# Flags by a line in DRAM, and an earlier third mask, in an adaLN block on one core

## What is computed

```python
mod = (silu(c) @ wmod).reshape(2, 6, 1, -1)          # c is [2, 512]
sa, ca, ga, sb, cb, gb = (mod[:, i] for i in range(6))
ga, gb = guarded(ga), guarded(gb)                     # sign(g) * max(|g|, 0.25)
h = layernorm(x) * (1 + ca) + sa
keep = mask.reshape(16, 32, 16, 32).sum((1, 3)) > 0   # one answer per 32x32 block
x = x + ga * (h @ (weight * expand(keep)).T)
h = layernorm(x) * (1 + cb) + sb
g = silu(h @ Wg.T * ag); u = h @ Wu.T * au            # 1376 inner features
x = x + gb * ((g * u) @ Wd.T * ad)
```

## Time and profile before

| | us |
|---|---|
| median of 3 runs (lowest, highest) | 177.42 (176.82, 177.63) |
| the profiled execution, its own time | 176.95 |
| its span (first to last instruction) | 175.2 |
| PE busy in the span | 168.9 (96%) |
| DVE, ACT, POOL busy | 100.1, 81.7, 29.8 |
| DMA traffic | 23.73 MB |

### The profile page before, as it was taken

One profiled execution on the slowest core, in us unless ns is written; L12 is line 12 of the kernel. 1 busy time (PEld: TensorE's weight loads), 2 busy tenths in 40 slices (PEclk: granted clock), 3 DMA queues, 4 the chain that ended last, 5 costly groups with the idle time before them and its releaser, 6 DMA issues.

```text
span 175.2 us, 2553 instructions
## 1 busy us (share of the span) xinstructions
PE 168.9 (96%) x899; PEld 128.8 (74%) x899; DVE 100.1 (57%) x204; ACT 81.7 (47%) x115; POOL 29.8 (17%) x40
## 2 busy tenths in 40 slices
PE   6889999999999999999999999999999999999992
PEld 6855555375568887887788888888888888888881
DVE  6776862894594998324755564427644213442574
ACT  3034002578996957756466443553435524352200
POOL 1333620591049320000000000006500000000000
PEclk9999999999999999999999999999999999999999
DMA  5999997999959402331300000001500000000014
GB/s 175 358 404 402 409 292 241 412 409 404 400 174 314 134 0 50 88 78 31 123 0 6 0 4 0 4 0 60 185 4 0 4 0 4 0 6 0 4 60 180
DMA packets 12389, 23.73 MB, mean 135 GB/s; under 512 B 2920, under 2 KB 5232, under 8 KB 11856
## 3 DMA queue, kind: packets, MB, share of 16 engines
q1 hardware_dynamic: 10864, 22.03, 34.7%
q10 hardware_dynamic: 1504, 1.39, 2.6%
HBM read 19.48 MB, written 2.10 MB: 123 GB/s over the span
## 4 chain that ended last, share of the span: by engine, by line
PE 79%; DMA 7%; SPq 6%; DVE 4%; POOL 1%; issue 1%; ACT 0%; DVEq 0%; POOLq 0%
PE bank L915 46%; PE bank L985 20%; PE bank L883 8%; DMA maskt<-in_att_mask 5%; DMA wffn<-wffn 2%; SPq L241 2%; PE bank L971 2%; PE bank L790 2%; PE bank L862 1%; SPq L263 1%; SPq L256 1%; SPq L250 1%; SPq L253 1%; POOL awork L343 1%; DVE wffn L562 1%
## 5 line engine op out<-in xcount | busy, mean ns | idle before, releaser
L915 PE MATMUL bank<-ht,whi_gu 128*128 128x512 f32 x352 | 83.6, 391 | 0.0
L915 PEld LDWEIGHTS bank<-ht,whi_gu 128*128 128x128 f32 x352 | 65.6, 188 | 13.9 <-issue 0.5
L678 DVE SCALAR_TENSOR_TENSOR awork<-bank,scal,awork 128x512 f32<-128x512 f32 x22 | 16.5, 751 | 50.6 <-PE bank L915 48.2
L985 PE MATMUL bank<-whi_dn,in_split 128*128 128x512 f32 x148 | 37.3, 391 | 0.0
L492 ACT ACTIVATE awork<-bank,scal 128x512 f32<-128x512 f32 x22 | 15.2, 690 | 46.0 <-PE bank L915 46.0
L985 PEld LDWEIGHTS bank<-whi_dn,in_split 128*128 128x128 f32 x148 | 27.6, 188 | 5.9
L883 PE MATMUL bank<-awork,wffn 128*128 128x512 f32 x64 | 31.1, 606 | 0.4 <-ACT wffn L421 0.2
L440 ACT ACTIVATE whi_gu<-wffn 128x1024 fp32r<-128x1024 f32 x22 | 23.3, 1058 | 6.9 <-PE bank L915 6.9
L883 PEld LDWEIGHTS bank<-awork,wffn 128*128 128x128 f32 x64 | 10.7, 190 | 9.9 <-issue 7.4
L687 DVE TENSOR_TENSOR in_split<-awork,in_split 128x512 fp32r<-128x512 f32 x21 | 16.5, 786 | 0.7
L433 ACT ACTIVATE junk<-wffn 128x1536 uint8<-128x1536 uint16 x11 | 16.2, 1477 | 0.9 <-DMA wffn<-in_w_down 0.9
(11 more groups left out here) (72 smaller groups left out, 113.6 us busy)
## 6 DMA issues: line engine op xcount, KB each, us to landing
wffn<-in_w_gu SPq DMA_DIRECT2D x10, 512.0 KB, 8.6
wffn<-in_w_down SPq DMA_DIRECT2D x10, 256.0 KB, 9.4
xt<-in_x SPq DMA_DIRECT2D x8, 256.0 KB, 6.4
modw<-in_mod_ln SPq DMA_DIRECT2D x4, 512.0 KB, 7.3
modw<-in_mod_gate SPq DMA_DIRECT2D x2, 1024.0 KB, 9.6
modw<-in_mod_ln SPq DMA_DIRECT2D x2, 1024.0 KB, 9.2
maskt<-in_att_mask SPq DMA_DIRECT2D x4, 256.0 KB, 8.1
awork<-in_att_w SPq DMA_DIRECT2D x4, 256.0 KB, 8.1
```

The costliest lines, as they stand in the source:

```text
L678: dve.scalar_tensor_tensor(inner[:, s % 2, :], bank[gu_bank(s, 1)][:, :], scal[:, c, 1:2], silu_g[:, s % 2, :], ALU.mult, ALU.mult).then_i ...
L915: return pe.matmul(bank[gu_bank(s, u)][:, :], w, h, start=(k == 0 and part == 0), stop=(k == KT - 1 and part == 1))
L985: last = pe.matmul(bank[4 + t][:, :], h, w, start=(c == 0 and part == 0), stop=(c == C - 1 and part == 1))
```

## The change

It has four parts.

1. SP loads mask 2 ahead of the last two x tiles. DVE sums it behind the first statistics of batch 1 and makes keep behind the second. PE's `mask_blocks(2)` stands behind the fourth product of k = 0 instead of the first of k = 1. POOL multiplies the weights of slice 2 ahead of batch 1's first deviation. Epsilon is added by DVE, inside `stats`, behind every second tile, for all norms.
2. ACT copies gate 0 ahead of modulation 4, and the first of the checks moves from behind modulation 7 to behind modulation 5. DVE makes the first layer's four gate products of batch 0 ahead of the second turned block.
3. The flags of groups 1 and 2 no longer go through PE. `flag_vector` runs in steps 2 and 5; SP writes the column to a line in DRAM (128 rows of 4 bytes), waits until it has landed, and reads the line back into one partition (512 bytes); DVE reduces that line to its maximum and compares it, in steps 3 and 6. PE's two flag sums go; its flag loads stay where they were. On SP the first of these pairs stands behind the weight chunks' loads and ahead of the 16 block moves, the second behind these moves and ahead of the gate line.
4. Step 1 has two checks instead of one, and step 5 none instead of one.

```diff
--- before.py
+++ after.py
@@ -61,7 +61,9 @@
 HALF = D // 2
 SHIFT = BLK + NB
 
-CHECKS_AT = {0: 1, 1: 1, 2: 1, 3: 1, 4: 1, 5: 1}
+CHECKS_AT = {0: 1, 1: 2, 2: 1, 3: 1, 4: 1}
+FLAG_VECTOR_AT = {2: 1, 5: 2}
+FLAG_READ_AT = {3: 1, 6: 2}
 
 GROUPS = [(0, 4), (4, C - HELD), (C - HELD, C)]
 GROUP_OF = [g for g, (a, b) in enumerate(GROUPS) for _ in range(a, b)]
@@ -119,7 +121,10 @@
         mhalf = sb("mhalf", [P, TT])
         chk = sb("chk", [P, C])
         flagv = sb("flagv", [P, len(GROUPS)])
+        flagrow = sb("flagrow", [1, len(GROUPS), P])
+        flagmax = sb("flagmax", [1, len(GROUPS)])
         flags = sb("flags", [1, len(GROUPS)], I32)
+        flag_line = nc.dram_tensor("flag_line", (len(GROUPS), P), F32, kind="Internal").ap()
 
         gates = maskt[:, :, :].bitcast(F32)
 
@@ -212,6 +217,9 @@
         flagv_ok = sem("flagv_ok")
         flag_done = sem("flag_done")
         flag_ok = sem("flag_ok")
+        d_flag_out = sem("d_flag_out")
+        d_flag_in = sem("d_flag_in")
+        flagmax_ok = sem("flagmax_ok")
         wgu_hi = sem("wgu_hi")
         wd_hi = sem("wd_hi")
         gate_mm = sem("gate_mm")
@@ -269,9 +277,11 @@
             load_ln1(2)
             load_mask(1)
             load_att(1)
-            for t in range(TT, NB * TT):
-                load_x(t)
+            load_x(TT)
+            load_x(TT + 1)
             load_mask(2)
+            load_x(TT + 2)
+            load_x(TT + 3)
             load_att(2)
             load_ln1(3)
             sp.dma_start(modw[:, 2, :, :], mod_gate[0]).then_inc(d_gate[0], 16)
@@ -299,11 +309,19 @@
                                  w_gu_tail).then_inc(d_ffn[c], 16)
                     sp.dma_start(wffn[0:FT, c, 2 * D:3 * D], w_down[c * P:F, :])\
                       .then_inc(d_ffn[c], 16)
+            def turn_flag(g):
+                sp.wait_ge(flagv_ok, g + 1)
+                sp.dma_start(flag_line[g], flagv[:, g:g + 1]).then_inc(d_flag_out, 16)
+                sp.wait_ge(d_flag_out, 16 * g)
+                sp.dma_start(flagrow[0:1, g, :], flag_line[g:g + 1, :]).then_inc(d_flag_in, 16)
+
+            turn_flag(1)
             sp.wait_ge(xn_ok, XN_FIRST + 3 * TT)
             for j in range(P // BLK):
                 for i in range(P // BLK):
                     sp.dma_start(modw[BLK * j:BLK * (j + 1), 1, :, i * P:(i + 1) * P],
                                  modw[BLK * i:BLK * (i + 1), 0, :, j * P:(j + 1) * P]).then_inc(d_blocks[j], 16)
+            turn_flag(2)
             sp.wait_ge(grow_ok, 1)
             for b in range(NB):
                 sp.dma_start(gate_line[b], grow[b * KT:(b + 1) * KT, :]).then_inc(d_line, 16)
@@ -329,9 +347,6 @@
             def inverse_deviation(q, half):
 
                 two = slice(2 * half, 2 * half + 2)
-                pool.wait_ge(stats_ok, TT * q + 2 * half + 2)
-                pool.tensor_scalar(veps[:, q, two], mv[:, q, two, 1], EPS, None, ALU.add)\
-                    .then_inc(veps_ok, 1)
                 pool.wait_ge(veps_ok, 2 * q + half + 1)
                 pool.tensor_tensor(rstd[:, q, two], veps[:, q, two], mhalf[:, 0:2], ALU.pow)\
                     .then_inc(rstd_ok, 1)
@@ -352,8 +367,8 @@
             inverse_deviation(0, 1)
             mask_weights(0)
             mask_weights(1)
+            mask_weights(2)
             inverse_deviation(1, 0)
-            mask_weights(2)
             inverse_deviation(1, 1)
             mask_weights(3)
             for b in range(NB):
@@ -461,13 +476,13 @@
             copy_rows(2)
             move_first(act, BY_SYNC + 4)
             modulate(3)
+            copy_gate(0, bank[6])
             modulate(4)
-            copy_gate(0, bank[6])
             copy_gate(1, bank[7])
             modulate(5)
+            check_chunk(next(check_at))
             modulate(6)
             modulate(7)
-            check_chunk(next(check_at))
             check_chunk(next(check_at))
             copy_rows(3)
             check_chunk(next(check_at))
@@ -532,6 +547,10 @@
                 dve.bn_stats(bns[:, q, t, :], xt[:, n % (NB * TT), :]).then_inc(bn_done, 1)
                 dve.wait_ge(bn_done, n + 1)
                 dve.bn_aggr(mv[:, q, t, :], bns[:, q, t, :]).then_inc(stats_ok, 1)
+                if t % 2:
+                    dve.wait_ge(stats_ok, n + 1)
+                    dve.tensor_scalar(veps[:, q, t - 1:t + 1], mv[:, q, t - 1:t + 1, 1], EPS, None, ALU.add)\
+                       .then_inc(veps_ok, 1)
 
             def normalise_half(half, tiles):
                 cols = slice(half * HALF, (half + 1) * HALF)
@@ -663,8 +682,15 @@
                    .then_inc(flagv_ok, 1)
 
             def read_flag(g):
-                dve.wait_ge(flag_done, g + 1)
-                dve.tensor_scalar(flags[0:1, g:g + 1], bank[3][0:1, 0:1], 0.0, None, ALU.is_gt)\
+                if g == 0:
+                    dve.wait_ge(flag_done, 1)
+                    top = bank[3][0:1, 0:1]
+                else:
+                    dve.wait_ge(d_flag_in, 16 * g)
+                    top = flagmax[0:1, g:g + 1]
+                    dve.tensor_reduce(top, flagrow[0:1, g, :], AX_X, ALU.max).then_inc(flagmax_ok, 1)
+                    dve.wait_ge(flagmax_ok, g)
+                dve.tensor_scalar(flags[0:1, g:g + 1], top, 0.0, None, ALU.is_gt)\
                    .then_inc(flag_ok, 1)
 
             def ffn_inner(s):
@@ -708,10 +734,10 @@
             mod_columns(1)
             keep_blocks(1)
             stats(1, 0)
+            sum_mask(2)
             stats(1, 1)
-            sum_mask(2)
+            keep_blocks(2)
             stats(1, 2)
-            keep_blocks(2)
             stats(1, 3)
             normalise(1)
             sum_mask(3)
@@ -722,9 +748,9 @@
             gate_sums(0)
             guard_gate(0)
             transpose_first(0)
-            transpose_first(1)
             for t in range(TT):
                 gate_linear(0, t)
+            transpose_first(1)
             transpose_first(2)
             transpose_first(3)
             for t in range(TT):
@@ -742,10 +768,10 @@
                 if s == 0:
                     for t in range(TT):
                         gate_linear(1, t)
-                for g, (first, _) in enumerate(GROUPS):
-                    if s == first - 1:
-                        flag_vector(g)
-                        read_flag(g)
+                if s in FLAG_VECTOR_AT:
+                    flag_vector(FLAG_VECTOR_AT[s])
+                if s in FLAG_READ_AT:
+                    read_flag(FLAG_READ_AT[s])
                 ffn_inner(s)
                 if s == 0:
                     stats(3, 0)
@@ -895,8 +921,6 @@
 
             def flag_sum(g):
                 pe.wait_ge(flagv_ok, g + 1)
-                if g == 2:
-                    pe.wait_ge(grow_ok, 1)
                 pe.matmul(bank[3][0:1, 0:1], flagv[:, g:g + 1], onecol[:, :], start=True, stop=True)\
                   .then_inc(flag_done, 1)
 
@@ -1060,7 +1084,7 @@
                 (0, 0): [rows_second],
                 (0, 1): [lambda: columns(1), lambda: mask_blocks(1)],
                 (0, 2): [lambda: transposes(2)],
-                (1, 0): [lambda: mask_blocks(2)],
+                (0, 3): [lambda: mask_blocks(2)],
                 (1, 1): [lambda: transposes(3)],
                 (2, 1): [rows_third, lambda: mask_blocks(3)],
                 (2, 2): [lambda: columns(2)],
@@ -1101,9 +1125,6 @@
                     gate_up_first()
                 else:
                     gate_up(s)
-                for g in range(1, len(GROUPS)):
-                    if s == GROUPS[g][0] - 1:
-                        flag_sum(g)
                 if LAG <= s < STEPS - HELD + LAG:
                     down(s - LAG)
                 if s == 5:
```

## The result

The changed kernel takes 189.61 us (median of 6 runs, 186.95 to 190.33) against 177.52 for the kernel before on the same chip. The ratio of 1.059 (interval 1.051 to 1.066) leaves out three of the six runs, 190.04, 190.06 and 190.33, which count as slow; with them the medians alone would give 1.068. So the change costs 10 to 12 us where 0.2 was forecast. The profiled execution is the quickest of the six: 186.95 us, span 185.1, 9.9 more than the 175.2 of before. The trace explains these 9.9. How the other runs spend their further 1 to 3 us was not traced; their mean granted clock is lower, 0.960 to 0.980 against 0.982.

What follows compares the result with a forecast made beforehand. PE's run without a gap from 31.54 us was taken as the bound; −0.1 + 0.6 + 0 − 0.3 = +0.2 us gave 177.15 for the profiled run, 177.6 us for the median, range 176.4 to 178.7.

Steps and rivals of the forecast that it cites:

- What bounds the kernel: PE works seemingly without a gap from 31.54 us; starting sooner or removing work pays, an added wait costs.
- The removed 0.43 and 0.3: Flag sums taken off PE in the two flag steps: −0.43 for the second flag, −0.3 taken for the third.
- part 3: Second flag, ahead of step 4: sum removed, −0.43, against a 0.38 gap from the DRAM round trip; net −0.05, say 0.
- Rival B: DRAM round trip becomes PE's wait at step 4, once write and read exceed 4.3 us; +1.15, 178.6 us; 20%.
- The race: Second flag needed by 67.35 to cost PE nothing at step 4; forecast at 67.75, a gap of 0.38.
- Part 4: Third flag: sum off PE, −0.3; line back at 83.4, branch done at 84.95, ahead of 85.4, so hidden.
- Part 1: Third mask, epsilon and POOL's order: normalisation ends at 22.0 instead of 22.11; −0.1 us, bounds 0.5 sooner, 0.3 later.
- Part 2: Order around first gate: check ahead of modulations 6 and 7 delays the fourth copy of rows to 41.93; +0.6 us.
- PE's reaction to a flag: PE's load, register operation, assert and branch, ending 1.1 us behind the flag.

Runs made afterwards that it cites:

- e8: Kernel before with second and third flags by one transfer inside SBUF, second flag's vector and reading sooner, no changed front; 176.34 us, ratio 0.994.
- e2: Kernel before with only the diff's flag parts (two flags by the line in DRAM, checks' new steps); 186.73 us, ratio 1.052.
- e9: Kernel after with its second flag back on PE, only the third through the line in DRAM; 185.06 us, ratio 1.042.
- e10: e1_front_only with the 1 MB load of mod_ln2[0] issued behind SP's block moves instead of ahead of them; 181.09 us in one run.
- e5: Kernel before with only ACT's and DVE's new order around the first gate; 177.50 us against 177.60, ratio 1.0005.
- e1_front_only: Kernel after with its second and third flags back on PE, the rest of the change kept; 177.76 us against 177.38, ratio 1.001.
- e3: Kernel after with the flag's column copied straight into one partition's row in SBUF, without the line in DRAM; 176.85 us, ratio 0.996.

## Why the prediction was wrong, point by point

**What bounds the kernel** was read rightly: PE's run from 31.5 us on, in which a wait is paid in full. The removed 0.43 and 0.3 are real; e8, which removes both sums and puts no wait in their place, is 0.6% faster, about 1 us.

**The step that failed** is in part 3: "I take 1.9 for the write (nearest the block move) and 1.8 for the read", with 2.1 + 2.3 as their ends. The write took 7.7 and 7.3, the read 3.3 and 3.2. The nearest row was chosen by the count of rows, 128, and the other candidate by the target, DRAM. Neither shares the property that decides: all 128 words lie in one line. No row of before showed a transfer whose descriptors write into the same 512 bytes, and the upper end should then have been open, not a few tenths above the nearest row. Rival B's sentence "Against: the DMA engines are idle then" was no argument either: they were idle, and the write took 7 us. The race itself was laid out rightly, with its deadline and DVE's arrival. The point at which it decides is given as 4.3 us for both transfers; by the prediction's own times it is about 3.6 (DVE is free at 67.2, the write is issued at 63.5, and 0.1 lies between). Against either stand 11.0. Rival B, with 178.6, had the mechanism and the sign and lacked the size.

The figure of about 2.0 us of the Trainium skill (DMA: Bandwidth & Descriptors, Anatomy of one DMA) would not have helped. The Trainium skill gives it there for transfers issued from GpSimd. These are issued from SP, and small transfers on the idle queue took 1.1 to 2.1 us here when nothing stood in their way, and the write to one line 7. The Trainium skill (DMA: Bandwidth & Descriptors, Specifications) says that below 512 bytes the DMA engines do a read-modify-write. By itself that is not the price: 4 bytes in places 64 bytes apart took 1.40, as quick as the 1.54 of full rows. That such read-modify-writes of one line wait for one another would fit the writes of every run; it was not shown by itself.

**A term was missing**: the clock. PE idle for 7.5 us lost the higher clock, and the 16 products behind it took 1.65 longer (3.0 in e2). A range for a wait on PE has to hold this too once the wait is long.

**Part 4** said "Hidden". With 7.3 + 3.2 the flag came 1.8 late even in the shelter of the first gap, and 5.7 late without it (e9). That SP may reach the write only behind its 16 moves (79.87 in e9) was seen, and priced by the same wrong 3.7.

**Part 1** said −0.1; that the effect was so small is luck, as two errors cancel. POOL and DVE gained 0.8, not 0.1: both powers took 1.44 together and began at 18.64, so DVE started at 19.38 and not at 19.8. But "It reaches everything behind it: block moves" was wrong: SP issued the moves 0.8 sooner, and they landed no sooner (the first turned block at 29.94, 29.93 before). That the 1 MB load ahead of them sets their landing is what e10 points to (2 us each without it, 3.8 to 4.9 for SP's with it), in one execution.

**Part 2** said +0.6; e5 has 0. The chain itself was right, 4.7 us from the chunk to the end of the copy in the kernel after (36.36 to 41.08), in e5 (36.24 to 40.96) and in e10. The sum took the moment of the landing (37.20) from one execution as a constant. The check waited until 36.24 in e5, 36.36 in the kernel after, 37.59 in e1_front_only, where PE was late by more than that itself, and 40.36 in e10, where PE did wait 2.58 for the copy. The landing varies by more than the 0.6 that was worked out from it.

**PE's reaction to a flag** was given 1.1 us, up to the end of the branch. From the end of the flag's comparison to the next weight load it is 68.73 to 70.08 = 1.35 in e3 and 74.99 to 76.33 = 1.34 in the kernel after: mis-sized by 0.25.

## What to carry to other kernels

To turn a column of 128 partitions into a row, copy it inside SBUF, or give every word in DRAM its own 64 bytes, the one distance tried in the kernel; a line that many descriptors write word by word costs microseconds to write and again to read. When no row of a profile shows the operation, ask what the addresses have in common before choosing the nearest row, and leave the upper end open; measure it alone on an idle queue of the old kernel first. And price a long wait of PE with the clock that it loses.

## What the runs showed that was not expected

- 128 writes of 4 bytes into one DRAM line of 512 bytes take 6.7 to 7.7 us, against 1.4 to 1.7 when they are 64 bytes apart. In the kernel after the packets are over after 1.05 us; it is the completions that come late, one after the other.
- The first reading of that line afterwards takes 2.6 to 3.4 us, though the write has reported its completion, and the second 1.17.
- A packet of the instruction queue seems to have held up one part of a small transfer by 2 us (512 bytes apart: 15 of 16 semaphore steps by 1.39 us, the last at 3.31).
- The waits for the two flags cost 10 us together, and the second costs 7.7 alone, since SP's order makes it late by itself.
